# Transposing the normalised rows with one DVE instruction and a trip through DRAM, in place of PE transposes and sixteen small DVE transposes

## What is computed

```
def _layernorm(x, axis=-1, eps=1e-05):
    m = jnp.mean(x, axis=axis, keepdims=True)
    v = jnp.var(x, axis=axis, keepdims=True)
    return (x - m) / jnp.sqrt(v + eps)

x = x + _L0_attn_ref(_layernorm(x))   # linear attention, 16 heads, phi = silu + 1
x = x + _L0_ffn_ref(_layernorm(x))    # silu(x w1)*(x w2), two gelu layers of 1024, w3; ternary weights
x = x + _L1_attn_ref(_layernorm(x))   # softmax attention, one head of 256
x = x + _L1_ffn_ref(_layernorm(x))    # tanh(((x W) A1) A2 + b)
```

## Time and profile before

| | |
|---|---|
| runs | 1982.26, 1982.6, 1984.07 us, median 1982.6 |
| span of the profiled execution | 1981.5 us |
| PE, PEld busy | 1961.9, 1895.6 us (99%, 96%) |
| DVE, ACT, POOL busy | 1289.0, 1020.0, 406.8 us (65%, 51%, 21%) |
| DMA queues in the body | 0.03 of the 16 engines in one pass |
| granted clock of PE | 0.996 of full speed on the mean |

### The profile page before, as it was taken

One profiled execution on the slowest core, in us unless ns is written; L12 is line 12 of the kernel. 1 busy time (PEld: TensorE's weight loads), 2 busy tenths in 40 slices (PEclk: granted clock), 3 DMA queues, 4 the chain that ended last, 5 costly groups with the idle time before them and its releaser, 6 DMA issues.

```text
span 1981.5 us, 37810 instructions
## 1 busy us (share of the span) xinstructions
PE 1961.9 (99%) x15288; PEld 1895.6 (96%) x15288; DVE 1289.0 (65%) x3292; ACT 1020.0 (51%) x1786; POOL 406.8 (21%) x344
## 2 busy tenths in 40 slices
PE   8999999999999999999999999999999999999998
PEld 7999999999999999999999999999999999999996
DVE  6546768566685665767667676666856667676357
ACT  3445545555554655455554455555546454554433
POOL 1112212212122021311213121121220213112121
PEclk9999999999999999999999999999999999999999
DMA  9600000000000000000000000000000000000000
GB/s 359 224 3 1 22 1 12 11 2 22 1 22 1 1 22 1 22 1 1 22 1 22 1 1 22 1 22 1 23 1 1 22 1 12 1 1 12 1 1 23
DMA packets 24538, 46.03 MB, mean 23 GB/s; under 512 B 1264, under 2 KB 21488, under 8 KB 24176
## 3 DMA queue, kind: packets, MB, share of 16 engines
q1 hardware_dynamic: 24352, 43.41, 6.1%
HBM read 35.02 MB, written 19.92 MB: 28 GB/s over the span
## 4 chain that ended last, share of the span: by engine, by line
PE 97%; DMA 1%; DVE 1%; SPq 1%; issue 0%; ACT 0%; POOL 0%; DVEq 0%; ACTq 0%
PE ffn_fill L1117 49%; PE att_fill L1048 25%; PE ffn_fill L1048 13%; PE ffn_fill L1174 6%; PE att_fill L1136 1%; PE att_fill L1252 1%; DMA scratch_w2T<-in_w2T 1%; DMA w<-scratch_w1T 0%; SPq L543 0%; PE ffn_fill L1285 0%; DVE late_sm L869 0%; PE ffn_fill L1280 0%; ACT late_kv_b L1009 0%; DVE st L671 0%; DVE late_prob_t_lo L864 0%
## 5 line engine op out<-in xcount | busy, mean ns | idle before, releaser
L1117 PE MATMUL ffn_fill<-act_hi,h 128*128 128x256 f32 x4096 | 987.2, 283 | 0.8 <-issue 0.2
L1117 PE MATMUL ffn_fill<-act_lo,h 128*128 128x256 f32 x4096 | 978.2, 280 | 1.2 <-issue 1.2
L1117 PEld LDWEIGHTS ffn_fill<-act_hi,h 128*128 128x128 f32 x4096 | 770.3, 188 | 9.2 <-POOL act_lo L649 3.9
L1117 PEld LDWEIGHTS ffn_fill<-act_lo,h 128*128 128x128 f32 x4096 | 773.1, 189 | 3.6
L976 ACT ACTIVATE whole<-ffn_fill,scales 128x256 f32<-128x256 f32 x512 | 214.0, 469 | 291.3 <-PE ffn_fill L1117 290.1
L649 POOL TENSOR_TENSOR act_lo<-whole,act_hi 128x512 fp32r<-128x512 f32 x128 | 166.8, 1303 | 492.4 <-DVE act_hi L798 492.4
L802 DVE TENSOR_TENSOR act_lo<-whole,act_hi 128x512 fp32r<-128x512 f32 x256 | 183.4, 716 | 112.0 <-ACT act_hi L980 109.7
L1048 PE MATMUL ffn_fill<-half_hi,w 128*128 128x256 f32 x1024 | 245.9, 283 | 0.0
L1048 PE MATMUL ffn_fill<-half_lo,w 128*128 128x256 f32 x1024 | 244.3, 281 | 0.0
L1048 PEld LDWEIGHTS ffn_fill<-half_lo,w 128*128 128x128 f32 x1024 | 193.3, 189 | 0.1
L1048 PEld LDWEIGHTS ffn_fill<-half_hi,w 128*128 128x128 f32 x1024 | 192.5, 188 | 0.4 <-issue 0.2
(11 more groups left out here) (239 smaller groups left out, 3277.8 us busy)
## 6 DMA issues: line engine op xcount, KB each, us to landing
x<-in_L_attn_x SPq DMA_DIRECT2D x16, 512.0 KB, 3.3
out<-x SPq DMA_DIRECT2D x15, 512.0 KB, 2.9
h<-scratch_h1T SPq DMA_DIRECT2D x2, 2048.0 KB, 13.1
h<-scratch_h2T SPq DMA_DIRECT2D x2, 2048.0 KB, 13.4
w<-scratch_w1T SPq DMA_DIRECT2D x1, 1024.0 KB, 7.8
w<-scratch_w2T SPq DMA_DIRECT2D x1, 1024.0 KB, 9.8
w<-scratch_w3T SPq DMA_DIRECT2D x1, 1024.0 KB, 8.3
rows<-in_rows SPq DMA_DIRECT2D x1, 640.0 KB, 5.5
```

The costliest lines, as they stand in the source:

```text
L1117: last = pe.matmul(two(bank)[:, o, :], view(w), view(moving[:, k, :]), start=k == 0 and o == 0 and half == 0, stop=k == KH - 1 and half == ...
```

## The change

In the body (and for `n:NT0` of the FIRST part), every turn takes one new form. DVE makes one transpose over all 128 partitions (128x1024, or 128x512 for a half tile), which turns each 32x32 square in place and leaves the squares where they were (`in_blocks`). SP then writes that tile to a DRAM scratch (`spread`), waits for it, and reads it back with four DMAs, one for each band of 32 partitions, in runs of 32 elements (128 bytes), which puts the squares in their places in `turned` (`placed`). ACT waits for `placed` and copies the high part. Both `c:LT` steps of the body become `c:T`, so POOL, not DVE, makes their `xt_lo`, and PE makes no transposes of normalised rows there. `in_blocks` lies over `qz_hi`, `turned` over `qz_lo`. SP gets an order of its own (`SP_ORDERS`). The layout of `turned` changes to [128, blocks, 2, 128], with views that follow. The FIRST and END parts keep their `LT` steps.

```diff
@@ BODY, PE_ORDERS
-    U0 U1 U2 U3 G0 G1a c:LT G1b c:CV c:CZ G2a c:CS0 G2b G3a c:CP0 c:CS1 c:CS2 G3b c:CO0 c:CP1 c:CS3 H0a
-    c:CO1 c:CP2 H0b c:CO2 c:CP3 H1 c:CO3 H2 H3 W0 U0 c:LT U1 U2 U3 c:CFa G0a c:CFb G0b G1 G2 G3 a:AKV0
-    a:AKV1 a:AKV2 a:AKV3 H0a a:AS a:AQ a:AM H0b H1a a:AO H1b H2 H3 W1"""),
+    U0 U1 U2 U3 G0 G1 G2 c:CV c:CZ G3a c:CS0 G3b H0a c:CP0 c:CS1 c:CS2 H0b c:CO0 c:CP1 c:CS3 H1a
+    c:CO1 c:CP2 H1b c:CO2 c:CP3 H2 c:CO3 H3 W0 U0 U1 U2 U3 G0 G1a c:CF G1b G2 G3a a:AKV0
+    a:AKV1 a:AKV2 a:AKV3 G3b a:AS a:AQ a:AM H0 a:AO H1 H2 H3 W1"""),
@@ BODY, DVE_ORDERS
-    c:CSTa U0 U1 U2 U3 c:CSTb c:CNO c:LT c:CQ c:CV c:CZ c:CS0 G0 c:CP0 c:CS1 c:CS2 c:CO0 G1 c:CP1 c:CS3 G2
-    G3 c:CO1 c:CP2 c:CO2 BST1 c:CP3 H0 BNO1 a:AST c:CO3 c:DSTa H1 c:DSTb NT1a H2 NT1b H3 NTL1 c:DNO W0 U0 U1
-    c:LT U2 U3 a:ANO c:CF a:Ta a:Tb G0 G1 a:AKV0 a:AKV1 G2 a:AKV2 a:AKV3 a:AS G3 a:AQ a:AM a:AO n:BST0 H0
-    n:BNO0 H1 n:NT0a H2 n:NT0b H3 n:NTL0 W1"""),
+    c:CSTa U0 c:CSTb U1 U2 c:CNO c:T U3 G0 c:CQ G1 G2 c:CV c:CZ c:CS0 G3 c:CP0 c:CS1 c:CS2 c:CO0 H0 c:CP1 c:CS3
+    BST1 c:CO1 c:CP2 BNO1 NT1 H1 c:CO2 c:CP3 a:AST H2 NTL1 c:CO3 c:DST H3 c:DNO c:T W0 U0 U1
+    a:ANO U2 a:T U3 G0 G1 c:CF G2 a:AKV0 a:AKV1 a:AKV2 a:AKV3 G3 a:AS a:AQ a:AM H0 a:AO n:BST0 H1
+    n:BNO0 n:NT0 H2 H3 n:NTL0 W1"""),
@@ BODY, ACT_ORDERS
-    U0 U1 U2 U3 c:LT G0 G1 c:CV c:CZ c:CS0 c:CP0 G2 c:CS1 c:CS2 c:CP1 G3 c:CS3 c:CP2 H0 c:CP3 H1 H2 H3 NT1
-    U0 U1 c:LT U2 U3 c:CF G0 a:T G1 G2 a:AKV0 a:AKV1 a:AKV2 a:AKV3 G3 a:AQ a:AM H0 H1 H2 H3 n:NT0"""),
+    U0 U1 U2 U3 G0 G1 c:T G2 c:CV c:CZ c:CS0 G3 c:CP0 c:CS1 c:CS2 H0 c:CP1 c:CS3 c:CP2 H1 c:CP3 H2 NT1 H3
+    U0 U1 U2 U3 G0 c:T G1 c:CF a:T G2 a:AKV0 a:AKV1 a:AKV2 a:AKV3 G3 a:AQ a:AM H0 H1 H2 H3 n:NT0"""),
+SP_ORDERS = {
+    "FIRST": order_from("FOLD0 n:NT0"),
+    "BODY": order_from("c:T NT1 c:T a:T c:CF n:NT0 W1"),
@@ BODY, POOL_ORDERS
-    U0 U1 U2 U3 c:CST c:CB BST1 a:AST c:DST U0 U1 U2 U3 c:CF a:T a:AB n:BST0"""),
+    U0 c:CST U1 U2 U3 c:T c:CB BST1 a:AST c:DST U0 U1 U2 U3 c:T c:CF a:T a:AB n:BST0"""),
@@ SP
+            def turn_blocks(c, made, free, whole, scratch, into, spread, placed):
+                nb = into.shape[1]
+                sp.wait_ge(s[made], c.value(made, 1))
+                wait(sp, s[placed], c.value(placed))
+                wait(sp, s[free], c.value(free))
+                sp.dma_start(scratch, whole[:]).then_inc(s[spread], 16)
+                sp.wait_ge(s[spread], c.value(spread, 16))
+                spots = scratch.rearrange("(q i) (m c j) -> c i m q j", i=SQ, c=P // SQ, j=SQ)
+                for there in range(P // SQ):
+                    rows_there = into[there * SQ:(there + 1) * SQ].rearrange("p b k (q j) -> p (b k) q j", j=SQ)
+                    sp.dma_start(rows_there, spots[there]).then_inc(s[placed], 16)
@@ DVE, T
-                    for there in range(P // 2 if share == "b" else 0, P // 2 if share == "a" else P, SQ):
-                        for here in range(0, P, SQ):
-                            ...
-                            last = dve.transpose(into[:, :, :, here:here + SQ], ...)
+                    wait(dve, s["spread"], c.value("spread"))
+                    dve.transpose(in_blocks[:], own.xn[:].rearrange("p b d -> p (b d)")).then_inc(s["turned"], 1)
@@ ACT, T
-                    act.wait_ge(s["turned"], c.value("turned", 1))
+                    act.wait_ge(s["placed"], c.value("placed", 64))
```

More of the change, by code:

```diff
@@ L87 @@
     "DNO": {"xn_ready": NB},
-    "T": {"turned": 1, "xt_hi_ready": 2, "xt_lo_ready": 2},
+    "T": {"turned": 1, "spread": 16, "placed": 64, "xt_hi_ready": 2, "xt_lo_ready": 2},
     "AKV": {"att_fill": 1, "k_silu": 1, "phik_ready": 1},
@@ L150 @@
 PLAN = steps_from("""
-    U0 c:CST U1 U2 U3 c:CNO G0 c:LT c:CB c:CQ G1 c:CV c:CZ G2 c:CS0 G3 c:CP0 c:CS1 c:CS2 c:CO0 c:CP1 c:CS3
-    H0 c:CO1 c:CP2 H1 c:CO2 BST1 c:CP3 BNO1 a:AST H2 c:CO3 c:DST H3 NT1 NTL1 c:DNO W0 c:LT a:ANO U0 U1 c:CF a:T
+    U0 c:CST U1 U2 U3 c:CNO G0 c:T c:CB c:CQ G1 c:CV c:CZ G2 c:CS0 G3 c:CP0 c:CS1 c:CS2 c:CO0 c:CP1 c:CS3
+    H0 c:CO1 c:CP2 H1 c:CO2 BST1 c:CP3 BNO1 a:AST H2 c:CO3 c:DST H3 NT1 NTL1 c:DNO W0 c:T a:ANO U0 U1 c:CF a:T
     U2 U3 a:AB a:AKV0 a:AKV1 a:AKV2 G0 a:AKV3 G1 G2 a:AS a:AQ a:AM G3 a:AO H0 H1 n:BST0 n:BNO0 H2 H3 n:NT0 n:NTL0
@@ L582, in _, with part @@
+            def part(step, c, slots):
+                kind, j, who = step
+                if kind == "FOLD":
                     wait_taken(sp, c, "att_fill", 0)
                     wait_taken(sp, c, "att_fill", 1)
[L584 to L597, removed]
-                else:
+                    for t in range(2, SLOTS):
+                        sp.dma_start(x[:, t], x_in[t]).then_inc(x_loaded[t], 16)
+                elif kind == "T":
+                    turn_blocks(c, "turned", "xt_lo_ready", in_blocks, a["scratch_turn"], turned, "spread", "placed")
+                elif kind == "NT":
+                    turn_blocks(c, "b_turned", "bt_lo", in_blocks_b, a["scratch_turn_b"], turned_b, "b_spread", "b_placed")
+                elif kind == "CF":
+                    t = c.value("out_ready")
@@ L601, in _ @@
+            walk(part, SP_ORDERS)
             sp.wait_ge(x_stored, 16 * (T - 1 + NB))
@@ L759, in part @@
                                 c.value(own.own + "xn_ready", c.ago(own.own + "xn_ready", norm, 0, who == "d") + NB))
-                    wait(dve, s["xt_lo_ready"], c.value("xt_lo_ready"))
-                    for there in range(P // 2 if share == "b" else 0, P // 2 if share == "a" else P, SQ):
-                        for here in range(0, P, SQ):
-                            into = turned[there:there + SQ].rearrange("p k (b n) -> p b k n", b=NB)
-                            last = dve.transpose(into[:, :, :, here:here + SQ],
-                                                 own.xn[here:here + SQ].rearrange("p b (k n) -> p b k n", k=KD)
-                                                 [:, :, :, there:there + SQ])
-                    if share != "a":
-                        last.then_inc(s["turned"], 1)
+                    wait(dve, s["spread"], c.value("spread"))
+                    dve.transpose(in_blocks[:], own.xn[:].rearrange("p b d -> p (b d)")).then_inc(s["turned"], 1)
                 elif kind == "BT":
@@ L774, in part @@
                     dve.wait_ge(s["xn_ready"], c.value("xn_ready", c.ago("xn_ready", "BNO", j) + HB))
[L775 to L783 removed]
+                    wait(dve, s["b_spread"], c.value("b_spread"))
+                    dve.transpose(in_blocks_b[:], xn_b[:].rearrange("p b d -> p (b d)")).then_inc(s["b_turned"], 1)
                 elif kind == "NTL":
                     dve.wait_ge(s["bt_hi"], c.value("bt_hi"))
[L786 removed]
+                    dve.tensor_tensor(half_by_block(half_lo), turned_b[:].rearrange("p b k n -> p k b n"),
+                                      half_by_block(half_hi).bitcast(F32), ALU.subtract).then_inc(s["bt_lo"], 1)
                 elif kind == "U":
```

48 lines of the change are left out of this document (26 added, 22 removed).

## The result

The changed kernel takes **2306.6 us** (median of 4 runs, 2305.6 to 2309.5) against 1983.3 us of the kernel before (1982.3 to 1984.1): a ratio of 1.163, 95% interval 1.162 to 1.165. The profiled execution has a span of 2303.0 us against 1981.5.

A forecast was written before the change was run, and what follows sets the result against it. PE was taken to bound the kernel, almost never waiting. Waits of 13.6 us a pass plus 1.7 for the clock less 1.74 saved gave 13.6, 190 in 14 passes: 2173 us, range 2085 to 2290.

The forecast's parts named there:

- six places: Points in a pass where PE would wait for late results: G0 of both halves, c:CV, c:CF, a:AKV0, U0; 13.6 us together.
- places 1 and 3: G0 of first and second half: U3's act_lo comes later behind DVE's added work; +2.5 and +2.2 us a pass.
- place 2: c:CV: xt_lo, now made by ACT behind G1 and by POOL, comes after PE's G2; +1.1 us a pass.
- place 4: c:CF: ACT has a table load and G0 ahead of the copies, while PE asks half of G1 after G0; +4.2 us.
- place 5: a:AKV0: POOL's xt_lo of a:T comes only behind the bias, tanh and add of c:CF; +3.2 us a pass.
- place 6: U0: n:NT0's way over DRAM ends after PE's demand; +0.4 us a pass (0 to 4, by the price of DRAM).
- softmax stretch: PE's halves of G and H cover it as before, costed at nothing; 1 us a pass if that cover fails.
- PE transposes: Two c:LT a pass leave PE at 0.87 us each, saving 1.74 us a pass, 24.4 us in all.
- clock: PE idle at c:CF drops to 1.2 GHz: one fall a pass counted, 1.7 us (0 to 3.4).
- W0 to W0: Growth of one pass: the waits and the clock less the saved transposes, 13.6 us, 190 in 14 passes.
- signs to watch: W0 distance near 134 us, act_lo and xt_lo waits, 1.2 us transpose, reads 5 to 6 us behind the write, clock below 0.99.
- rival of a slow DRAM: 128-byte packets cost like 1 KB ones, 19 us more a pass: 2440 us, at half that 2240 to 2300; chance 0.2.

The follow-up runs named there:

- x2: Changed kernel with idle matmuls given to PE at the five places where it waits, nothing others wait for moved; 2232.5 us (ratio 1.125).
- x1: Changed kernel with U3 (first half) and U2, U3 (second half) again ahead of statistics, normalisation and transposes on DVE; 2323.3 us.
- x3: Changed kernel without the trip over DRAM, squares left where DVE put them, so later rows are in the wrong order; 2301.4 us.
- x10: Changed kernel with the softmax stretch ordered as in the kernel before: c:CP1 ahead of H0's silu on ACT and H0's low part on DVE; 2294.7 us.
- x5: Changed kernel where, in the second half, ACT makes c:T's high parts ahead of G0 instead of behind it; 2228.4 us.
- x13: Changed kernel without the trip over DRAM (later rows in wrong order) and with U3, U2 ahead of statistics and transposes on DVE; 2198.4 us.
- x8: Changed kernel, second half: ACT makes c:T's high parts ahead of G0, ACT and POOL take a:T ahead of c:CF's tanh and add; 2166.8 us.
- x6: Mix: first half as in the kernel before; second half's c:T, made ahead of H3, a:T and half tiles over DRAM; 2065.3 us.
- x9: Kernel before with only the second half's c:T over DVE and DRAM, made ahead of W0; a:T and half tiles by small transposes; 2035.9 us.
- x7: Kernel before with the statistics' end and c:CNO ahead of U3 on DVE in the first half, c:LT still on PE; 2017.5 us.
- x11: Mixed kernel (first half as before; second half's c:T, a:T and half tiles over DRAM), with a:AKV0 asked for behind all of G3; 2030.4 us.
- x4: Kernel before with PE making only 2 of the 8 transposes of each c:LT in the body; 1963.7 us.
- x12: Kernel before with second half's c:T over DRAM, c:DNO behind H3, a:T's small transposes in their own tile, a:T ahead of c:CF's tanh and add; 1984.0 us.
- x14: Kernel before with second half's c:T (made ahead of H3) and NT1 over DRAM, a:T by small transposes in its own tile; 1979.8 us.

## Why the prediction was wrong

The direction and the six places were right, the size was not: 2306.6 against 2173, and above the range, which ended at 2290. The filled run (x2) gives the waits at full clock, by the same sums of matmul starts (its idle matmuls, 0.119 us each, counted with the place they fill); the clock is what the changed kernel has above it, 143.7 against 138.6 from W0 to W0. In us a pass:

```
term                       predicted   measured
G0, places 1 and 3            4.7         6.1
c:CV, place 2                 1.1         1.4
c:CF, place 4                 4.2         4.4
a:AKV0, place 5               3.2         3.7
U0 and half tiles, place 6    0.4         1.5
softmax stretch               0           2.4
PE transposes                -1.74       -1.76
other joints                  -           0.1
clock                         1.7         5.1
W0 to W0                     13.6        23.0
```

**The clock** is the largest single miss, 3.4 us a pass. "I count one such fall a pass" was the failing step: there were three, 40 in 13 passes. The price of one was right: 5.1 us a pass by 3.1 falls is 1.7 each. The row it came from the earlier trace rows showed what a fall costs, and not how many there would be; I had listed four waits of 2 to 4 us a pass and gave one of them a fall. That it is the clock is shown by x2. How many falls came with which waits, in 13 passes, with the half clock in brackets:

- x1, three waits of 3.5 to 7.1 us a pass: 38 falls (249 us).
- The changed kernel, three of 3.1 to 4.1 and three of 1.0 to 1.2: 40 (184 us). x3 and x10, with the same waits but for the short ones: 40 and 43 (212 and 218).
- x5, without the wait of c:CF: 30 (130 us); x13, one of 4.1, one of 3.5 and one of 1.0: 26 (171 us); x8: 23 (96 us).
- x6, one wait of 2.5 to 4.6: 12 (51 us).
- x9, one of 2.2 to 2.8 and one of 0.8: 7 (27 us).
- x7, one of 2.2: 1 (7 us). x11, waits of about 1: 1 (3 us). x4, x12 and x14: none.

So not every wait brings a fall, and no run here isolates which do.

**The softmax stretch**, 2.4. "PE's halves of G and H cover it as before" looked at PE's order alone. The orders of ACT and DVE had changed with it: H0 came in ahead of `c:CP1` on both, which x10 undid: the waits for `prob_t_lo` went. Even the price named there, 1 us if the cover fails, was under half.

**Places 1 and 3**, 1.4. `c:CNO` was taken at 1.38 from a row in which POOL was idle; in the new place POOL makes `act_lo`. At `a:ANO` I had taken 2.0 for the same instruction, between 1.38 alone and 2.35 beside POOL, and didn't ask for it here. x7 measures it at 2.34, and the wait at place 1 was 3.4 us in the changed kernel against the 2.5 of the sum.

**Place 6**, 1.1. About 1.0 of the 1.5 is the wait I had costed at 0.4, U0's for the low part of `n:NT0`; its trip takes a write of 2.0 us, four issues in 2.6, and a landing 2.5 us after an issue. Another 0.3 is a wait behind W0 that I hadn't listed: in some passes U1 waits up to 1.0 us for DVE's step of W0. x3, which has no trip, has neither.

**Places 2, 4 and 5** were right to 0.5 us each, and x5 and x8 show the mechanism of 4 and 5; for place 2 only the wait's size is seen. The saving of 1.74 was right as PE time.

**Edges.** The span grew by 321.5 us, and 13 intervals between W0 explain 299.4; what is ahead of the first W0 of the body and behind the last, which I took as one more pass of 13.6, grew by 8.9 and 13.3.

**Of the signs to watch**: the transposes' 1.24 us, the waits' places and the clock below 0.99 (0.95) came; the distance of two W0 was 143.7 and not 134; the last read landed 5.6 to 7.0 us behind the write, 6.0 in the middle, instead of 5 to 6. The rival of a slow DRAM was wrong as I put it (of the reads back, the only one for which ACT waited by more than a us in all is that of `half_hi`, 32.5 us in 29 waits). The trip still was what kept U3 from going first, the wait of place 1: x1 and x13 show that together, and no single removal does.

## What to carry to other kernels

When a tuned order is rewritten, add up the waits by place, and count a fall of the clock for each of the long ones, not one for all; here a wait of 2.2 us a pass brought next to none, and one to three waits of 3 us and more brought one to three a pass. Idle matmuls in the waits are a cheap way to measure that part. Follow every engine's order through a stretch, also where PE's own order seems unchanged, and take an instruction's duration from a row in which its neighbours are as busy as they will be. If removing a cost changes nothing, look for the order that was bent around it, and undo both at once.
